# GNN on one core: in the edge groups without counts, the highest score's broadcast and the exponentials move one group ahead of the weighting, and the order of work on ScalarE and TensorE changes

## The chip, the cores and the metric

One core of a Trainium2 chip runs the whole program in one launch. The metric is the device time in microseconds, median of the runs.

## The reference, cut to what matters

A graph attention layer over 6250 nodes and 200000 edges (sorted by destination), then a residual node update, then four graph convolutions over the same edges. The part around the change is the attention and the first nodes' update:

```
ft = (hn @ W_att).reshape(n, 10, 13)
scores = einsum('ehd,ehd->eh', ft[src], ft[dst]) / sqrt(13)
m = segment_max(scores, dst);  ex = exp(scores - m[dst])
z = segment_sum(ex, dst);      a = ex / z[dst]
agg = segment_sum(ft[src] * a[:, :, None], dst)
out = elu(agg) @ hr_w + hr_b + hn
out = layernorm(out); skip2 = out
out = elu(elu(out @ w1 + b1) @ w2 + b2) + skip2
```

## The kernel before

**Groups.** `attention` cuts the edges into 196 groups of 1024 (8 columns of 128). One loop body per engine is run for k = 0 to 195 plus LAG = 3 more (`steps`); each body works on several groups at once: `nxt` = k+1, `one` = k-1, `two` = k-2, `late` = k-3, `over` = k-4. I call body k "pass k". Engines meet at semaphores only, and each works through its own list in order. GpSimd gathers the source rows of a group with eight indirect DMAs into one of six `fts` buffers; the gathers of group n wait for the weighting of group n-6.

**What one group goes through.** TensorE: `nearness` (a distance between edge and node, one matmul), ScalarE: `destination_rows` (a Relu that makes the one-hot `ohdT`), TensorE: `closeness` (the same, turned, into the same PSUM bank), ScalarE: `destination_columns` (the one-hot `oh`), TensorE: `first_features` and `last_features` (rows of the destinations, `ftd_ps`), VectorE: `first_products`, `last_products` (product with the gathered rows, the reduction to scores, and the running highest score), TensorE: `turn_highest`, VectorE: `highest` (one number for the group), TensorE: `broadcast_highest` (to all partitions, `spread`), ScalarE: `numerators` (copy of the shift, Exp into PSUM, fade, Exp into `terms`), VectorE: `weighted` (gathered rows times exponentials), TensorE: `first_sums`, `later_sums`, `carried`, `last_sum` into `agg_ps`, ScalarE: `result`, and a store by SP.

**Two kinds of group.** Passes 0 to 175 (`counted`, k < NSD = 176) also count edges into the adjacency strips. Passes 176 to 198 have no counts; in their place they carry the fused update of the first 14 node tiles. That is cut into four units with 17 phases, `units_at(k, 0)` being the pieces in the first place of a pass and `units_at(k, 1)` those in the second; the units begin at slots 0, 5, 15, 20 of two slots a pass, so the last piece falls in pass 194. TensorE has work in phases 2, 3 (turns), 4 (`project`, three matmuls a tile), 7 (turn), 8 to 11 (`up`), 12 (`down`), 13 and 16 (turns). Behind each `up` ScalarE takes an Exp (`exp_cols`) and VectorE an elu (`elu_quarter`), and the next `up` needs that elu, since it uses the same bank. Phases 5 and 14 are `deviation` (a Sqrt on ScalarE, which needs another activation table than Exp) and `coefficients` on VectorE.

**Order within a pass without counts, before.** TensorE: broadcast of k-3, turn of k-2, nearness of k+1, first piece, closeness, first and later sums of k-3, last features of k-1, last sums of k-3, first features of k, second piece. ScalarE: numerators of k-3, destination rows of k+1, result of k-4, first piece, destination columns of k+1, second piece. VectorE, which isn't changed: weighting of k-3, first products of k-1, highest of k-2, first piece, last products of k-1, second piece.

Of the kernel before, what the change touches and what calls it, by code (L numbers as in the profile page):

```python
# [5 lines left out]
F32 = mybir.dt.float32  # L6
# [3 lines left out]
ACT = mybir.ActivationFunctionType  # L10
# [3 lines left out]
P = 128  # L14
# [56 lines left out]
NSD = T0 * P // SUB  # L71
# [705 lines left out]
def attention(nc, t, sb, pb, sem, g):  # L777
# [15 lines left out]
    LAG = 3  # L793
# [5 lines left out]
    with ExitStack() as c:  # L799
# [33 lines left out]
        s2T = [sb(f"fu_s2T{a}", [D, UW * P], F32, c) for a in range(2)]  # L833
        uT = [a[:].rearrange("p s n k -> p (s n k)").bitcast(F32)[:, 0:4 * UW * P].rearrange("p (f n) -> p f n", f=4)
              for a in (ohk, ohl)]
        st, mv = sb("fu_st", [P, 2, UW, 6], F32, c), sb("fu_mv", [P, 2, UW, 2], F32, c)
        sd, rs, nb = (sb("fu_" + n, [P, 2, UW], F32, c) for n in ("sd", "rs", "nb"))
        adj_ps = [pb(f"adj_ps{q}", [P, 512], F32, c) for q in range(2)]
# [52 lines left out]
        def units_at(k, half):  # L891
            slot = 2 * (k.n - SLOTS_AT) + half
            return [(Unit(i), slot - first) for i, first in enumerate(STARTS) if 0 <= slot - first < PHASES]
# [311 lines left out]
        def _(act):  # L1205
            act.wait_ge(iotas, 1)

            def low_distances(k):

                own = low_cols[:, k.n].rearrange("p a c -> p (a c)")  # L1210
                if k.after(2):
                    act.wait_ge(dist_l_done, k.n - 1)
                nc.scalar.copy(low[:, k.s, :], own[:, LD:NA * SC]).then_inc(lows_done, 1)  # L1213
                if k.after(1):
                    act.wait_ge(ohl_done, k.n)
                act.wait_ge(lows_done, k.n + 1)
                for n in range(NA * SC - LD):
                    last = nc.scalar.activation(dist_l[:, n, :], lo_iota[:], ACT.Abs, bias=low[:, k.s, n:n + 1], scale=-1.0)  # L1218
                last.then_inc(dist_l_done, 1)
# [22 lines left out]
            def numerators(k):  # L1242

                act.wait_ge(spread, k.n + 1)
                nc.scalar.copy(shift[:, k.s, :], most_ps[:, P:P + 2]).then_inc(shift_done, 1)
                act.wait_ge(shift_done, k.n + 1)
                if k.after(1):
                    act.wait_ge(terms_done, k.n)
                nc.scalar.activation(most_ps[:, EX_AT:EX_AT + GC * H], score[:, k.c, 0:GC * H], ACT.Exp,  # L1249
                                     bias=shift[:, k.s, 0:1], scale=RS).then_inc(exp_done, 1)  # L1250
                if k.after(1):
                    nc.scalar.activation(fade[:, k.s, 0:1], shift[0:WD, k.s, 0:1], ACT.Exp,
                                         bias=shift[0:WD, 1 - k.s, 1:2]).then_inc(fade_done, 1)
                if k.after(2):
                    act.wait_ge(agg_done, k.n - 1)
                nc.scalar.activation(terms[:, k.s, :, HD:HD + H],
                                     score[:, k.c, 0:GC * H].rearrange("p (c h) -> p c h", h=H), ACT.Exp,
                                     bias=shift[:, k.s, 0:1], scale=RS).then_inc(kept_done, 1)

            def result(k):  # L1260

                act.wait_ge(agg_done, k.n + 1)
                if k.after(UN):
                    act.wait_ge(agg_out, 16 * (k.n - UN + 1))
                nc.scalar.copy(res[:, k.u, :], agg_ps[0:WD, 0:WA]).then_inc(res_done, 1)
# [23 lines left out]
            def deviation(k, var, done):  # L1289
                act.wait_ge(var, k.i + 1)  # L1290
                nc.scalar.activation(sd[:, k.a, 0:k.w], mv[:, k.a, 0:k.w, 1], ACT.Sqrt, bias=eps[:]).then_inc(done, 1)

            def normal(k):
                act.wait_ge(f["nb1"], k.i + 1)
# [28 lines left out]
            def nodes(k, phase):  # L1323
                if phase == 1:
                    exp_attention(k)
                elif phase == 2:
                    copy_attention(k)
                elif phase == 3:
                    copy_rest(k)
                elif phase == 5:  # L1330
                    deviation(k, f["var1"], f["sd1"])
                elif phase == 6:
                    normal(k)
                elif phase == 7:
                    scaled_cols(k)
                elif 8 <= phase < 12:
                    exp_cols(k, f["up_ps"], 4 * k.i + phase - 7, b1[:, phase - 8:phase - 7], f["exF"])
                elif phase == 12:
                    exp_cols(k, f["v_ps"], k.i + 1, b2[:], f["exV"])
                elif phase == 14:  # L1340
                    deviation(k, f["var2"], f["sd2"])
                elif phase == 15:
                    rectified(k)
                elif phase == 16:
                    hT_out(k)

            def body(k):
                nxt, late, over = k.at(1), k.at(-LAG), k.at(-LAG - 1)
                if k.counted():
                    if k.after(2):  # L1350
                        act.wait_ge(strip_out[k.s], 16 * (k.j * (UN // 2) + k.u // 2))
                    copy_quarter(k, 0)
                if late.exists():
                    numerators(late)
                if nxt.exists():
                    destination_rows(nxt)
                if k.counted():
                    copy_quarter(k, 1)
                if over.exists():
                    result(over)  # L1360
                for unit, phase in units_at(k, 0):
                    nodes(unit, phase)
                if nxt.exists():
                    destination_columns(nxt)
                for unit, phase in units_at(k, 1):
                    nodes(unit, phase)
                if k.counted():
                    copy_quarter(k, 2)
                if nxt.counted():
                    low_distances(nxt)  # L1370
                    low_one_hots(nxt)
                if k.counted():
                    copy_quarter(k, 3)
                    act.wait_ge(strip_done, 4 * k.n + 4)
                    act.dma_start(adj[k.n],
                                  strip[:, k.s].rearrange("p t a d -> p (t a d)")).then_inc(strip_out[k.s], 16)
            zero = Group(0)
            low_distances(zero)
            low_one_hots(zero)
# [5 lines left out]
        def _(pe):  # L1385
# [83 lines left out]
            def later_sums(k):  # L1469
                add_terms(k, range(HC, GC - 1))  # L1470
# [80 lines left out]

            def body(k):
                nxt, one, two, late = k.at(1), k.at(-1), k.at(-2), k.at(-LAG)
                if late.exists():
                    broadcast_highest(late)
                if two.exists():
                    turn_highest(two)
                def last_sums():
                    if late.after(1):
                        carried(late)  # L1560
                    last_sum(late)

                def counted():
                    count(k, 0)
                    if nxt.exists():
                        nearness(nxt)
                    count(k, 1)
                    count(k, 2)
                    if one.exists():
                        last_features(one)  # L1570
                    if nxt.exists():
                        closeness(nxt)
                    count(k, 3)
                    if late.exists():
                        first_sums(late)
                        later_sums(late)
                    first_features(k)
                    if late.exists():
                        last_sums()

                def uncounted():
                    if nxt.exists():
                        nearness(nxt)
                    for unit, phase in units_at(k, 0):
                        nodes(unit, phase)
                    if nxt.exists():
                        closeness(nxt)
                    first_sums(late)
                    later_sums(late)
                    if one.exists():  # L1590
                        last_features(one)
                    last_sums()
                    if k.exists():
                        first_features(k)
                    for unit, phase in units_at(k, 1):
                        nodes(unit, phase)
                if k.counted():
                    counted()
                else:
                    uncounted()  # L1600
# [1233 lines left out]
```

## Time and profile before

| | |
|---|---|
| median of 3 runs | 3775.62 us (3770.89 to 3781.33) |
| profiled execution, its time | 3790.5 us |
| its span | 3788.6 us |
| mean granted TensorE clock | 0.892 |
| busy: PE, DVE, ACT, POOL | 89%, 62%, 47%, 65% |
| gathers of the attention stage (L1001) | 118.5 to 2076.4 us |

The stages stand one behind the other with a barrier between: a prelude to about 118 us, attention to about 2118 us, the rest of the node update, and the convolutions from between 2250 and 2300 us. Times in the trace count from the start of the span; a line number is that of the kernel before.

### The profile page before, as it was taken

To read this page: it belongs to the slowest core of one execution; us is meant where nothing else is said; L and a number is where in the kernel's file an instruction comes from. 1 tells how busy PE (TensorE), PEld (TensorE's weight loads), DVE (VectorE), ACT (ScalarE), POOL (GpSimd) and SP (SyncE) were. 2 spreads that over 40 slices of the span, in tenths; PEclk is the share of its full clock that TensorE was granted. 3 is DMA by queue.
4 is the path that set the end of the run, shared out by engine and by line. 5 is a ranking of instruction groups with operands and counts; after the bars stand their busy time and mean duration, and the time that the engine had idled before them with its cause. 6 is when DMAs were issued, how large, how long until landed. Compare 5 with 4: busy or idle time off the path is not lost. (4 is left out here: it accounts for less than half of the span.)

```text
span 3788.6 us, 59184 instructions
## 1 busy us (share of the span) xinstructions
PE 3354.5 (89%) x20346; PEld 2097.6 (55%) x20346; DVE 2355.1 (62%) x3512; ACT 1776.8 (47%) x4853; POOL 2445.6 (65%) x2604
## 2 busy tenths in 40 slices
PE   5788888888888888888888787999999999999999
PEld 4566666666666666666655554444544454445444
DVE  8788888888888888888865574222422242224223
ACT  4788888888888878787744353000200020002000
POOL 2577777777777777777777001777277737764775
PEclk7688888888888888888887798999999999999999
DMA  7443334333333333334332415888688868877886
GB/s 207 125 108 103 107 104 107 104 107 104 107 104 107 104 107 104 107 104 124 103 85 60 62 51 169 254 254 256 215 255 254 253 215 254 256 248 229 259 264 192
DMA packets 491674, 599.98 MB, mean 158 GB/s; under 512 B 61546, under 2 KB 422613, under 8 KB 491103
## 3 DMA queue, kind: packets, MB, share of 16 engines
q1 hardware_dynamic: 355798, 337.71, 29.3%
q0 software_dynamic: 82960, 172.57, 18.4%
q10 hardware_dynamic: 52632, 86.13, 6.3%
q8 instruction: 152, 2.49, 0.3%
q14 instruction: 132, 1.07, 0.1%
HBM read 488.79 MB, written 109.00 MB: 158 GB/s over the span
## 5 line engine op out<-in xcount | busy, mean ns | idle before, releaser
L1001 POOL DMA_INDIRECT fts<-ft_tab,src_all x1568 | 1481.2, 945 | 477.7 <-issue 477.1
L2702 PE MATMUL cv_acc<-cv_cnt,cv_parts 128*128 128x512 bf16 x3960 | 864.0, 379 | 0.0
L2453 POOL DMA_INDIRECT cv_slots<-hs_tab,slot_idx x640 | 604.8, 945 | 195.1 <-issue 195.1
L1033 DVE TENSOR_TENSOR ohk<-iota_ps,key_cols 128x784 bf16<-128x784 f32 x704 | 651.1, 966 | 5.5
L2702 PEld LDWEIGHTS cv_acc<-cv_cnt,cv_parts 128*128 128x128 bf16 x3960 | 387.2, 98 | 464.6
L1457 PE MATMUL agg_ps<-terms,oh 128*64 128x141 f32 x2744 | 557.1, 378 | 75.6 <-DVE terms L1070 75.3
L1457 PEld LDWEIGHTS agg_ps<-terms,oh 128*64 128x64 f32 x2744 | 483.2, 189 | 116.3 <-DVE terms L1070 105.4
L1218 ACT ACTIVATE dist_l<-lo_iota,low 128x128 bf16<-128x128 f16 x1760 | 533.1, 387 | 16.5 <-ACT low L1213 0.4
L1397 PE MATMUL adj_ps<-ohk,ohl 128*128 128x196 bf16 x2816 | 378.2, 261 | 89.5 <-ACT strip L1270 46.8
L1270 ACT CAST strip<-adj_ps 128x392 bf16<-128x392 f32 x704 | 334.0, 474 | 239.5 <-PE adj_ps L1400 200.4
L2702 PE MATMUL cv_acc<-raw,cv_parts 128*128 128x512 bf16 x1920 | 420.9, 379 | 0.0
L1047 DVE TENSOR_TENSOR prod<-ftd_ps,fts 128x780 f32<-128x780 f32 (+1 forms) x392 | 271.0, 691 | 225.9 <-DMA fts<-ft_tab,src_all 198.4
L1423 PE MATMUL ftd_ps<-win,ohdT 64*128 64x130 f32 x3136 | 325.8, 334 | 77.7 <-DVE prod L1047 76.4
L2453 POOL DMA_INDIRECT spare<-hs_tab,slot_idx x320 | 302.6, 946 | 97.5 <-issue 97.5
L1397 PEld LDWEIGHTS adj_ps<-ohk,ohl 128*128 128x128 bf16 x2816 | 215.2, 100 | 221.7 <-DVE ohk L1033 109.5
L1423 PEld LDWEIGHTS ftd_ps<-win,ohdT 64*128 64x128 f32 x3136 | 244.3, 219 | 157.3 <-DVE prod L1047 90.1
L2702 PEld LDWEIGHTS cv_acc<-raw,cv_parts 128*128 128x128 bf16 x1920 | 187.7, 98 | 226.7
L2669 ACT ACTIVATE cv_sd<-cv_mv,eps 128x1 f32<-128x1 f32 x2 | 0.6, 294 | 662.0 <-DVE cv_tmp L2620 662.0
L2514 DVE TENSOR_REDUCE spare<-cv_slots 128x128 f32<-128x1152 f32 x50 | 106.5, 2130 | 303.0 <-DMA cv_slots<-hs_tab,slot_idx 302.9
L1070 DVE TENSOR_TENSOR terms<-fts,most_ps 128x1040 f32<-128x1040 f32 x196 | 240.9, 1229 | 21.5 <-ACT most_ps L1249 21.2
L1083 DVE TENSOR_REDUCE score<-prod 128x80 f32<-128x1040 f32 x196 | 242.4, 1237 | 6.7
L1225 ACT ACTIVATE ohl<-dist_l 128x1280 bf16<-128x1280 bf16 x176 | 223.5, 1270 | 16.3 <-ACT dist_l L1218 0.4
(350 smaller groups left out, 3592.1 us busy)
## 6 DMA issues: line engine op xcount, KB each, us to landing
cv_cnt<-adj SPq DMA_DIRECT2D x44, 2176.0 KB
cv_cnt<-adj SPq DMA_DIRECT2D x44, 2048.0 KB
raw<-adj SPq DMA_DIRECT2D x44, 2048.0 KB
adj<-strip ACTq DMA_DIRECT2D x176, 392.0 KB
fts<-ft_tab,src_all POOLq DMA_INDIRECT x1568
win<-ft_tab SPq DMA_DIRECT2D x196, 65.0 KB
hs_tab<-cv_hs ACTq DMA_DIRECT2D x24, 448.0 KB, 3.5
cv_slots<-hs_tab,slot_idx POOLq DMA_INDIRECT x640
```

The source lines that it names most:

```text
L1001: nc.gpsimd.indirect_dma_start(fts[u][:, k, :], None, ft_tab[:, :], bass.IndirectOffsetOnAxis(src_all[:, n, k:k + 1], 0)).then_inc(gathere ...
L1033: nc.vector.tensor_tensor(ohk[:, k.s, at, :], key_no.unsqueeze(1).to_broadcast([P, QC, KEYS]), columns(key_cols, k)[:, at].unsqueeze(2).to ...
L1047: nc.vector.tensor_tensor(by_half(prod[:]), ftd_ps[:, :, 0:n * HD].rearrange("p a (c f) -> p a c f", f=HD), by_half(fts[k.f][:]), ALU.mult ...
L1070: nc.vector.tensor_tensor(terms[:, k.s, :, 0:HD].rearrange("p c (h d) -> p c h d", d=DH), fts[k.f][:].rearrange("p c (h d) -> p c h d", d=DH),
L1083: nc.vector.tensor_reduce(score[:, k.c, 0:GC * H], prod[:].rearrange("p c (h d) -> p (c h) d", d=DH), AX.X, ALU.add).then_inc(score_done, 1)
L1218: last = nc.scalar.activation(dist_l[:, n, :], lo_iota[:], ACT.Abs, bias=low[:, k.s, n:n + 1], scale=-1.0)
L1270: nc.scalar.copy(strip[:, k.s, :, QS * q:QS * (q + 1), :].rearrange("p t a d -> p a t d"), adj_ps[q % 2][:, 0:QS * KEYS].rearrange("p (a t ...
L1397: nc.tensor.matmul(counts_ps[:, a * KEYS:(a + 1) * KEYS], ohl[:, k.s, n, :], ohk[:, k.s, n, :], start=(a == 0 and m == 0), stop=False)
L1423: last = nc.tensor.matmul(ftd_ps[:, half, m * HD:(m + 1) * HD], ohdT[at, k.u, (c0 + m) * P:(c0 + m + 1) * P], win[at, k.u, :], start=True, ...
L1457: nc.tensor.matmul(agg_ps[0:WD, 0:WA], oh[:, k.o, col, half, :], terms[:, k.s, n, :], start=(n == 0), stop=False)
L2453: nc.gpsimd.indirect_dma_start(slots[n % RING][:, e, :], None, hs_tab[:, :], bass.IndirectOffsetOnAxis(rows_at, 0)).then_inc(slots_in[n % ...
L2702: last = nc.tensor.matmul(a[:, 0:width], parts[:, r, b, :], cnt[q][:, 0:width // SUB, (b - b0) * SUB:(b - b0 + 1) * SUB], start=(b == 0 an ...
```

## The change

In passes without counts only: TensorE broadcasts the highest score of group k-2 in pass k, behind the sums and the first piece, and ScalarE makes that group's numerators in pass k between the two pieces. Pass 176, the first of its kind, does both group 173 and group 174. On ScalarE the destination rows come first, then the result and the destination columns, then the first piece. On TensorE closeness follows nearness, then the first and later sums, the first piece, the broadcast, the last features, the last sums, the second piece, and the first features. An Exp on one column (`warm`) follows each Sqrt of `deviation`. Passes with counts keep their order; VectorE, GpSimd and SP are as before.

```diff
--- before.py
+++ after.py
@@ -833,6 +833,7 @@
         s2T = [sb(f"fu_s2T{a}", [D, UW * P], F32, c) for a in range(2)]
         uT = [a[:].rearrange("p s n k -> p (s n k)").bitcast(F32)[:, 0:4 * UW * P].rearrange("p (f n) -> p f n", f=4)
               for a in (ohk, ohl)]
+        warm = sb("fu_warm", [P, 1], F32, c)
         st, mv = sb("fu_st", [P, 2, UW, 6], F32, c), sb("fu_mv", [P, 2, UW, 2], F32, c)
         sd, rs, nb = (sb("fu_" + n, [P, 2, UW], F32, c) for n in ("sd", "rs", "nb"))
         adj_ps = [pb(f"adj_ps{q}", [P, 512], F32, c) for q in range(2)]
@@ -1289,6 +1290,7 @@
             def deviation(k, var, done):
                 act.wait_ge(var, k.i + 1)
                 nc.scalar.activation(sd[:, k.a, 0:k.w], mv[:, k.a, 0:k.w, 1], ACT.Sqrt, bias=eps[:]).then_inc(done, 1)
+                nc.scalar.activation(warm[:], eps[:], ACT.Exp)
 
             def normal(k):
                 act.wait_ge(f["nb1"], k.i + 1)
@@ -1345,35 +1347,46 @@
                     hT_out(k)
 
             def body(k):
-                nxt, late, over = k.at(1), k.at(-LAG), k.at(-LAG - 1)
-                if k.counted():
+                nxt, two, late, over = k.at(1), k.at(-2), k.at(-LAG), k.at(-LAG - 1)
+
+                def counted():
                     if k.after(2):
                         act.wait_ge(strip_out[k.s], 16 * (k.j * (UN // 2) + k.u // 2))
                     copy_quarter(k, 0)
-                if late.exists():
-                    numerators(late)
-                if nxt.exists():
+                    if late.exists():
+                        numerators(late)
                     destination_rows(nxt)
-                if k.counted():
                     copy_quarter(k, 1)
-                if over.exists():
-                    result(over)
-                for unit, phase in units_at(k, 0):
-                    nodes(unit, phase)
-                if nxt.exists():
+                    if over.exists():
+                        result(over)
                     destination_columns(nxt)
-                for unit, phase in units_at(k, 1):
-                    nodes(unit, phase)
-                if k.counted():
                     copy_quarter(k, 2)
-                if nxt.counted():
-                    low_distances(nxt)
-                    low_one_hots(nxt)
-                if k.counted():
+                    if nxt.counted():
+                        low_distances(nxt)
+                        low_one_hots(nxt)
                     copy_quarter(k, 3)
                     act.wait_ge(strip_done, 4 * k.n + 4)
                     act.dma_start(adj[k.n],
                                   strip[:, k.s].rearrange("p t a d -> p (t a d)")).then_inc(strip_out[k.s], 16)
+
+                def uncounted():
+                    if k.n == NSD:
+                        numerators(late)
+                    if nxt.exists():
+                        destination_rows(nxt)
+                    result(over)
+                    if nxt.exists():
+                        destination_columns(nxt)
+                    for unit, phase in units_at(k, 0):
+                        nodes(unit, phase)
+                    if two.exists():
+                        numerators(two)
+                    for unit, phase in units_at(k, 1):
+                        nodes(unit, phase)
+                if k.counted():
+                    counted()
+                else:
+                    uncounted()
             zero = Group(0)
             low_distances(zero)
             low_one_hots(zero)
@@ -1551,7 +1564,7 @@
 
             def body(k):
                 nxt, one, two, late = k.at(1), k.at(-1), k.at(-2), k.at(-LAG)
-                if late.exists():
+                if late.exists() and k.n <= NSD:
                     broadcast_highest(late)
                 if two.exists():
                     turn_highest(two)
@@ -1581,19 +1594,20 @@
                 def uncounted():
                     if nxt.exists():
                         nearness(nxt)
-                    for unit, phase in units_at(k, 0):
-                        nodes(unit, phase)
-                    if nxt.exists():
                         closeness(nxt)
                     first_sums(late)
                     later_sums(late)
+                    for unit, phase in units_at(k, 0):
+                        nodes(unit, phase)
+                    if two.exists():
+                        broadcast_highest(two)
                     if one.exists():
                         last_features(one)
                     last_sums()
+                    for unit, phase in units_at(k, 1):
+                        nodes(unit, phase)
                     if k.exists():
                         first_features(k)
-                    for unit, phase in units_at(k, 1):
-                        nodes(unit, phase)
                 if k.counted():
                     counted()
                 else:
```

## Rows read from the trace of the kernel before

**Rows 1.** The page, the granted clock in 40 equal slices of the span, in tenths of full speed.
```profile
PEclk7688888888888888888887798999999999999999
```

**Rows 2.** One line's instructions: duration min/median/max in ns, first and last start.
```profile
L1001 POOL DMA_INDIRECT fts<-ft_tab,src_all x1568: 940/944/1278, 118.5 to 2076.4; - x196
```

**Rows 3.** Timeline of VectorE (start, us, engine, line, operation [idle before <-releaser]).
```profile
1918.06 0.97 DVE L1047 TENSOR_TENSOR prod<-ftd_ps,fts 128x780 f32<-128x780 f32 x1 [2.67 <-DMA fts<-ft_tab,src_all]
...
2098.36 0.95 DVE L1047 TENSOR_TENSOR prod<-ftd_ps,fts 128x780 f32<-128x780 f32 x1
```

**Rows 4.** Stretches: length, busy us of PE, PEld, DVE, ACT, POOL, clock, DMA, GB/s.
```profile
1918.10:2114.70 196.60, 166.48 (x934) 112.78 (x934) 114.66 (x244) 80.07 (x196) 120.84 (x127) 0.79 0.29 68
...
1945.10:1956.60 11.50, 10.10 (x63) 5.93 (x62) 9.22 (x24) 5.20 (x11) 8.76 (x10) 1.00 0.43 108
...
1992.60:2006.80 14.20, 11.93 (x58) 8.22 (x56) 6.63 (x18) 9.07 (x21) 10.85 (x12) 0.50 0.27 64
```

**Rows 5.** Waits of TensorE from 1918 to 2115 (us in total, times, longest).
```profile
PE agg_ps L1457 <- DVE terms L1070: 6.8, 6, 1.9
PE near_ps L1415 <- ACT ohdT L1233: 6.3, 4, 2.2
PE ftd_ps L1423 <- DVE prod L1047: 4.9, 5, 1.8
...
PE adj_ps L1518 <- DVE ohl L1141: 2.7, 3, 1.4
...
PE adj_ps L1518 <- DVE ohk L1141: 1.6, 2, 0.9
...
PE adj_ps L1524 <- DVE ohk L1141: 1.1, 1, 1.1
...
PE adj_ps L1524 <- DVE ohl L1141: 0.9, 1, 0.9
```

**Rows 6.** Timeline, the steps of the loop without a piece.
```profile
1885.34 0.39 PE L1410 MATMUL near_ps<-rows,spots 5*128 5x512 f16 x1
...
1885.78 0.58 ACT L1233 ACTIVATE ohdT<-near_ps 128x512 f32<-128x512 f32 x1
...
2094.04 0.58 PE L1423 MATMUL ftd_ps<-win,ohdT 64*128 64x130 f32 x4
...
2095.30 0.94 PE L1423 MATMUL ftd_ps<-win,ohdT 64*128 64x130 f32 x12
...
2096.17 0.38 PE L1444 MATMUL most_ps<-signs,most 1*128 1x2 f32 x2
...
2096.44 0.24 DVE L1088 TENSOR_REDUCE score<-score 128x1 f32<-128x81 f32 x1
...
2098.43 1.91 PE L1457 MATMUL agg_ps<-terms,oh 128*64 128x141 f32 x14 [1.32 <-DVE terms L1070]
...
2107.04 0.62 PE L1475 MATMUL agg_ps<-res,move 64*1 64x140 f32 x2
...
2108.13 0.38 PE L1444 MATMUL most_ps<-signs,most 1*128 1x2 f32 x2
```

**Rows 7.** Timeline, an up piece and its elu, and fourteen sums at half clock.
```profile
1961.71 1.12 PE L1518 MATMUL adj_ps<-fu_s2T,spare 128*128 128x512 f32 x2
...
1964.06 0.75 DVE L1141 SCALAR_TENSOR_TENSOR ohl<-adj_ps,spare,ohk 128x512 f32<-128x512 f32 x1
...
1905.41 3.55 PE L1457 MATMUL agg_ps<-terms,oh 128*64 128x141 f32 x14
```

**Rows 8.** ScalarE: groups of table loads from 1878 to 2112, and one in the timeline.
```profile
L1291 ACT ACT_TABLE_LOAD x8 | 10.3, 1283 | 0.1
...
L1249 ACT ACT_TABLE_LOAD x4 | 5.1, 1283 | 0.1
...
1902.24 1.28 ACT L1249 ACT_TABLE_LOAD   x1
...
1903.54 0.33 ACT L1249 ACTIVATE most_ps<-score,shift 128x80 f32<-128x80 f32 x1
```

## The prediction

> **What bounds the kernel now.** I read the profile's page first: the granted clock of TensorE swings over the attention stage, the first 22 of 40 slices, and is steady behind it [rows 1]. The edit touches only the groups without counts, so I looked for that stretch: groups 176 to 195 and three passes of the loop behind them. The gathers on GpSimd come first: 1568 of them, the first at 118.5 us and the last at 2076.4 us, with hardly a wait for anything but their own queue [rows 2]. That is 1957.9 / 1567 = 1.25 us each, 10.0 us for a group's eight. While a pass of the loop takes under 10 us, gathers set its rhythm. Then I followed the first products of each group on VectorE. Those of group 179 wait for their gather and start at 1918.06. Those of group 195 could start 0.7 us behind the last gather (1918.06 against 1917.4 is that 0.7: 16 groups of 10.0 us back from 2077.3), at 2078.0, but start at 2098.36 [rows 3]. In 16 passes the loop has fallen **20.3 us** behind, and what bounds the kernel from 1918.1 to the end of the last copy of `res` at 2114.7 [rows 4] is the ring of TensorE, ScalarE and VectorE, not the gathers. Those 20.3 us, and 1.1 us behind the last group (below), are all that an order of work can win.
>
> Of these 196.6 us TensorE is busy for 166.5 us, at a mean granted clock of 0.79 of 2.4 GHz. Single passes stand at 1.00 (11.5 us for one with a `down`) and others at 0.50 (14.2 us for the one from 1992.6) [rows 4]. It is idle for 196.6 - 166.5 = 30.1 us. The list of waits names most of that: 6.8 us for the weighted terms, 6.3 us for `ohdT`, 4.9 us for the products, and 2.7 + 1.6 + 1.1 + 0.9 = 6.3 us for the elu pieces of VectorE [rows 5].
>
> **The change, part by part.** No matmul goes or comes; TensorE's 166.5 us stay, and only idle time can move. I count in passes 181 to 194 (14 of them), where the loop is late.
>
> *Highest score and exponentials a group ahead.* `broadcast_highest` used to open the pass. From it to the first sum 2098.43 - 2096.17 = 2.26 us go by (copy of the shift, exponentials, weighting) [rows 6]. Now the exponentials of group k-2 are there before pass k+1 begins, so the wait for the terms in this form is gone: **6.8 us won**. Behind the last group, its last sums (8.13 - 7.04 us, carried row included) fit between broadcast and weighting instead of standing ahead of the broadcast: **1.1 us won** (2107.04 and 2108.13 are starts in [rows 6]).
>
> *`destination_rows` first on ScalarE.* It no longer stands behind the three exponentials and their table load: **6.3 us won**. But `closeness` now follows `nearness` at once, with nothing between. Nearness starts at 1885.34, the Relu at 1885.78 for 0.58 us: with 0.05 us to wake TensorE, closeness can't start before 1.07 us, of which nearness itself fills about 0.35 [rows 6]. That is 0.7 us idle in each of 14 passes, which before lay under the pieces or under the exponentials: **9.8 us lost**.
>
> *Pieces of the fused node update behind the sums.* Nearly the whole pass's sums now lie between the second piece of one pass and the first of the next, so the 6.3 us of waits for the elu at those places go, and with `first_features` behind the second piece also the 4.9 us for the products: **11.2 us won**. The price is at the other side. First and second piece now have only the broadcast (0.3 us), the last features and last sums (2095.30 - 2094.04 = 1.26 us, so 1.5 us in all) between them, while the way through ScalarE and VectorE takes from the end of an up piece (1961.71 + 1.12 = 1962.83) to the end of the elu (1964.81), 2.0 us, and 2.1 with the wake-up [rows 6, 7]: 0.6 us in the nine late passes in which both places hold such a piece (181 to 184, 188 to 192): **5.4 us lost**. VectorE's order is unchanged, so the elu of the first piece delays the last products, score and its maximum, and these gate `turn_highest`, which now has no broadcast ahead of it: from the last features 2096.44 + 0.24 - 2094.04 = 2.64 us, against 2.07 us of last sums and first features [rows 6]: 0.6 us where no second piece covers it, in about five passes: **3.0 us lost**. And the elu of the second piece stands on VectorE ahead of `weighted`: 2.1 + 1.24 us from that piece's end to the terms, against first features 0.87, a turn of about 0.3, 1.07 from nearness to closeness and closeness about 0.4, 2.6: 0.7 us in eight passes: **5.6 us lost**.
>
> *The `warm` activation.* The number of table loads stays: each of the eight at `deviation` is followed by one back, four of these ahead of the exponentials (5.1 us, [rows 8]); that one now follows at once. Where `deviation` is a first piece, ScalarE has nothing else to do: nothing, under the sums (1.9 us and more). As second piece it now puts 2 x 1.28 us of loads, the Sqrt and the Exp (0.33 us at most, as the wider one of 128x80 in [rows 8]), some 3.1 us, ahead of the next Relu. The four-matmul project covers that in pass 185, in 188 and 190 first features, turn and nearness (some 1.5 us) and the 0.7 already counted cover it only in part, and ScalarE also has an elu's Exp (0.69) there: I take 2.1 us for 188, where the Exp stands ahead of the loads, and 0.6 for 190, where it stands behind them and the broadcast's own 1.3 us overlap: **2.7 us lost**. If the last features covered it too, nothing.
>
> What a switch of tables costs is read from one of these loads: it starts at 1902.24, and the Exp behind it at 1903.54, so 1.3 us with everything [rows 8]. The Trainium skill (ScalarE: Activation LUTs, What ACT_TABLE_LOAD costs) counts a drain on top, 2.66 us in all. The trace disagrees, and decides. By the page the four loads ahead of exponentials would weigh some 5 us more before and those in passes 188 and 190 some 3 us more after, and the sum would fall by about 2 us.
>
> **The sum.** Won 6.8 + 1.1 + 6.3 + 11.2 = 25.4 us, lost 9.8 + 5.4 + 3.0 + 5.6 + 2.7 = 26.5 us: +1.1 us. Against the profiled execution (3790.5 us, span 3788.6) that is 3791.6. That execution is 14.9 us above the median of the runs, all of it in stages that I can't tell apart, so I carry the difference over: 3775.6 + 1.1 = **3776.7**, say 3777 us. The ends of the unknown terms: if the losses that I inferred from order alone (5.4, 3.0, 5.6, 2.7) were nothing, the sum is -15.6 us; if each were double, +17.8 us.
>
> **Rivals.**
> *The ring catches up (faster).* The 25.4 us are won, the new waits fall together, and TensorE, with no stop of over 1 us, holds 2.4 GHz: the pass from 1992.6 stood at half clock [rows 4], where 14 sums take 3.55 against 1.91 us [rows 6, 7]. Then the loop is as fast as the gathers: 20.3 + 1.1 us off, 3754; half of that is 3765. For: the waits are named in the profile. Against: a new wait lies ready behind each. Chance 0.17.
>
> *VectorE in order plus the clock (slower).* `weighted` and the last products stand behind elu pieces; stops of 2 us appear in passes 182 to 185, of which the one shown ran at 1.00 before, and the granted clock falls there to 0.50. A pass then costs 3.55 - 1.91 = 1.6 us more in its sums [rows 6, 7], and its other matmuls on the ring (last features and sums 1.26, first features 0.87, a piece 1.12, closeness 0.4: 3.65 us), lengthened in the same proportion and taken at two thirds of it since parts of them are covered, 2.1 us: 3.7 us, in three or four passes 11 to 15 us: 3788 to 3792. [...] For: the pass at 0.50 from 1992.6 has one of TensorE's waits of up to 2.2 us for `ohdT` ahead of it, behind a table load [rows 4, 5]. Against: the first sums follow at once. Chance 0.13.
> The Trainium skill (TensorE: Matmul & The Clock Gate, HAM oscillation — how this bites in real kernels) says that bursts of matmuls with waits between are run throttled again and again. The pass at 0.50 bears that out; by this rule the slower case would be the likely one.
>
> *It does nothing to the ring.* If the passes depend only on TensorE's own work and the waits just change their names, only the 1.1 us at the end remain: 3774.5. Chance 0.10, no change in any measurement.
>
> **How the numbers follow.** Forecast 0.60, nothing 0.10, faster 0.17, slower 0.13. Over 0.3%, 11.3 us, is what this kernel can tell from no change. So faster 0.17, same 0.70, slower 0.13. The range leaves a tenth at each end: down to half way into the catching-up case (3763), up to the lower end of the slower one (3789). The likeliest case alone is 3767 to 3786.
>
> **What would show it.** Right: the first products of group 195 still start 15 to 25 us behind the last gather; TensorE waits in the list for `ohdT` in nearly every pass, about 0.7 us each; the wait of `agg_ps` for terms is still there, now behind elu pieces; no table load stands at the exponentials' line; ring time from broadcast to first sum is no longer fixed at 2.3 us. The gathers still end within 1 us of 2077.3. Wrong: the last gather's group is multiplied within 8 us of its landing (the ring was won), or the granted clock of 1945 to 1980 is below 0.8 and the stage ends behind 2126 (slower case). A difference outside 1870 to 2120 us would mean something that I haven't seen.

## The result, and the profile after

The changed kernel takes 3792.9 us (median of 6 runs, 3787.6 to 3795.4) against 3776.4 us: ratio **1.0042, 95% interval 1.0028 to 1.0055**. It is slower by 16.4 us, beyond the upper end of the range (3789) and 1 us above the price of the slower rival (3788 to 3792). Ratios leave out single executions far above all others (4015 us of the kernel before, 10449 us of e13_more_filler, 5878 us of e15_ahead_filler).

The page of the changed kernel shows the granted clock of [rows 1] at this grain but for the first slice, and a span only 1.4 us longer than the 3788.6 us of the trace that the prediction rests on:

```profile
span 3790.0 us, 59192 instructions
...
PEclk8688888888888888888887798999999999999999
```

So the comparison of these two traces shows less than a tenth of the difference of the medians. That is the first thing to explain. Gathers, one line of the changed kernel (it is [rows 2] one line further down), with what they waited for:

```profile
L1002 POOL DMA_INDIRECT fts<-ft_tab,src_all x1568: 939/945/1203, 117.1 to 2079.9; - x196
...
  DVE terms L1071: 5.9, 3
```

The last gather starts 3.5 us later than before, and three gathers now wait 5.9 us in all for a buffer (two waited 0.6 us before): the loop has fallen back as far as six buffers allow. VectorE's first products of groups 179 and 195, and the last copy of `res`, in the timeline (as [rows 3]):

```profile
1917.82 0.95 DVE L1048 TENSOR_TENSOR prod<-ftd_ps,fts 128x780 f32<-128x780 f32 x1
...
2104.66 0.96 DVE L1048 TENSOR_TENSOR prod<-ftd_ps,fts 128x780 f32<-128x780 f32 x1
...
2117.38 0.27 ACT L1266 COPY res<-agg_ps 64x141 f32<-64x141 f32 x1 [3.38 <-PE agg_ps L1494]
```

The first products of group 195 start at 2104.66, 6.3 us later than before, and the copy ends at 2117.65 instead of 2114.65: from group 195's products to the end it is 13.0 us instead of 16.3. The end of the chain became shorter, the passes before it longer.

Stretches of the changed kernel (columns as in [rows 4]): group 180's first products to the end, two passes with fused pieces early on, and one at half clock:

```profile
1931.50:2117.68 186.18, 152.27 (x880) 101.56 (x877) 106.30 (x227) 81.73 (x196) 109.42 (x115) 0.83 0.27 64
1942.43:1959.57 17.14, 13.67 (x63) 8.34 (x63) 8.96 (x23) 6.02 (x12) 12.97 (x14) 0.80 0.37 88
1959.57:1972.64 13.07, 10.18 (x49) 6.15 (x49) 7.90 (x18) 6.96 (x17) 9.93 (x11) 0.76 0.42 99
...
2007.23:2019.19 11.96, 11.89 (x50) 8.00 (x50) 5.25 (x11) 2.84 (x9) 9.15 (x10) 0.50 0.31 65
```

TensorE is idle for 186.18 - 152.27 = 33.9 us of the first. Its waits, from 1918 to 2118 (as [rows 5]):

```profile
PE near_ps L1428 <- ACT ohdT L1234: 13.9, 15, 2.7
PE agg_ps L1470 <- DVE terms L1071: 11.4, 13, 1.9
PE agg_ps L1464 <- DVE score L1089: 3.8, 6, 1.4
PE ftd_ps L1436 <- DVE prod L1048: 2.0, 1, 2.0
...
PE adj_ps L1531 <- DVE ohk L1142: 1.0, 2, 0.6
PE adj_ps L1531 <- DVE ohl L1142: 0.9, 2, 0.5
PE adj_ps L1537 <- DVE ohl L1142: 0.6, 1, 0.6
```

The waits for `ohdT` doubled (6.3 to 13.9 us), those for terms went from 6.8 to 11.4, those for the maximum from 1.2 to 3.8. The waits for elu pieces shrank from 6.3 to 1.0 + 0.9 + 0.6 = 2.5 us and those for products from 4.9 to 2.0; that they shrink was forecast. How a pass comes to take 17.1 us is seen in its timeline:

```profile
1941.21 1.23 DVE L1071 TENSOR_TENSOR terms<-fts,most_ps 128x1040 f32<-128x1040 f32 x1
1941.74 0.60 PE L1428 MATMUL near_ps<-spots,rows 5*128 5x128 f16 x4 [1.85 <-ACT ohdT L1234]
...
1942.50 3.55 PE L1470 MATMUL agg_ps<-terms,oh 128*64 128x141 f32 x14 [0.15 <-DVE terms L1071]
...
1945.98 4.87 PE L1537 MATMUL adj_ps<-ohk,spare 128*128 128x512 f32 x8
...
1957.31 0.39 PE L1428 MATMUL near_ps<-spots,rows 5*128 5x128 f16 x4 [0.69 <-ACT ohdT L1234]
...
1958.36 1.23 DVE L1071 TENSOR_TENSOR terms<-fts,most_ps 128x1040 f32<-128x1040 f32 x1
```

Closeness (L1428) has waited 1.85 us for the Relu and starts at 1941.74. The sums (L1470) follow in 3.55 us: half clock, as in [rows 7]. The `down` behind them (L1537) takes 4.87 us. With the clock up again, closeness starts again at 1957.31, the weighting stands on VectorE behind the second piece's elu until 1958.36, and the next sums start only at 1959.64.

### The profile page after: what moved, and what is told of

It reads as the page before. It is cut to its first block and busy times, and to the rows that moved or that the text cites. A ratio compares the mean times of both kernels' runs of the same rounds, so it can differ in the third digit from the quotient of the medians.

```text
span 3790.0 us, 59192 instructions
## 1 busy us (share of the span) xinstructions
PE 3352.7 (88%) x20346; PEld 2093.9 (55%) x20346; DVE 2353.7 (62%) x3512; ACT 1782.7 (47%) x4861; POOL 2446.4 (65%) x2604
## 5 line engine op out<-in xcount | busy, mean ns | idle before, releaser
L1470 PE MATMUL agg_ps<-terms,oh 128*64 128x141 f32 x2744 | 556.9, 378 | 77.0 <-DVE terms L1071 77.0
L1470 PEld LDWEIGHTS agg_ps<-terms,oh 128*64 128x64 f32 x2744 | 483.2, 189 | 118.1 <-DVE terms L1071 106.8
L1226 ACT ACTIVATE ohl<-dist_l 128x1280 bf16<-128x1280 bf16 x176 | 223.5, 1270 | 16.3 <-ACT dist_l L1219 0.4
```

The lines of the kernel that those rows point to most:

```text
L1470: nc.tensor.matmul(agg_ps[0:WD, 0:WA], oh[:, k.o, col, half, :], terms[:, k.s, n, :], start=(n == 0), stop=False)
```

## The experiments

**A second trace of each kernel.** The kernel before, without an edit (e1_before), and the changed one (e2_after).

> The kernel before, once more, for a second trace: the profiled execution of before (3790.5 us) lies 14 us above its own median, so its trace may not show the typical run. Theory A (the change costs what the order of work costs, 10 to 16 us within passes 176 to 198): the ratio is 1.000, and if this trace is of a run near 3776 us, group 195's first products start 10 to 15 us earlier than the 2098.4 us of the first trace. Rival B (the loss lies outside the edited stretch, by the layout of memory or code): group 195's first products stay near 2098 us, and the 14 us lie elsewhere.

> The changed kernel once more. Both theories: ratio about 1.004. Theory A: its first products of group 195 again start at 2104 to 2110 us, and the last copy of res ends at 2117 to 2123. Rival B: those times move little, and a later stage is longer than in before.

The kernel before against itself, 12 runs: 1.0013 (1.0001 to 1.0025), 3771.9 to 3793.7 us: that interval misses 1, so differences of 0.1% mean nothing here. Its trace again was from a longer execution (3785.3 us), with passes equal to the first trace's within 0.1 us. The changed kernel: 1.0035 (1.0022 to 1.0048), five runs within 2.5 us; last copy of `res` from 2114.8. It repeats (11 runs within 8 us), and the kernel before does so less: its runs spread over 26 us.

**What the spread of the kernel before is.** No edit again (e10_before, e11_before).

> The kernel before, for one more trace. Its runs lie between 3767 and 3794 us, both traces so far at 3785 and 3790, and over 50 runs a lower mean granted clock goes with a longer time. If the clock in the late passes makes the difference: a trace near 3770 us ends its attention stage 10 to 15 us earlier than 2114, with fewer passes at 0.50. If another stage does, this trace's passes are as long as in the first.

> As e10_before: one more trace of the kernel before, to have traces from both ends of its spread.

They took 3775.3 and 3773.5 us, one execution each, and end their last copy at 2096.6 and 2098.9. The stretch from group 180's first products to the end, in the first trace:

```profile
1934.27:2114.68 180.41, 151.92 (x880) 103.17 (x879) 106.99 (x227) 77.67 (x189) 108.36 (x114) 0.81 0.28 65
```

and in that of e10_before:

```profile
1927.86:2096.58 168.72, 138.31 (x875) 94.53 (x875) 106.88 (x227) 76.99 (x189) 112.39 (x118) 0.90 0.31 71
```

The same matmuls take 138.3 us at a mean clock of 0.90 and 151.9 us at 0.81 (875 and 880 records of them), and idle time differs by 2 us (30.4 and 28.5). The rest of the kernel, from the end of that stretch to the end of the span, is 1673.9 us in the first trace, 1676.8 in e10_before and 1672.3 in the changed kernel's. So the 14.9 us between my trace and the median lay in the late passes, and rival B falls: the loss is in the edited stretch. Over 117 runs of the kernel before, time and mean granted clock correlate at -0.8; the fastest quarter has its median at 3770.7 us and 0.898, the slowest at 3784.5 and 0.894.

These traces also correct what bounds the kernel. The first products of group 195 in e10_before:

```profile
2078.49 0.97 DVE L1047 TENSOR_TENSOR prod<-ftd_ps,fts 128x780 f32<-128x780 f32 x1
```

Its last gather starts at 2075.1 and ends 0.9 us later, so by the prediction's reckoning (0.7 us behind the gather's end) these products are 1.8 us late, and those of e11_before also 1.8 us (2081.2 against 2079.4). The 20.3 us of the first trace belong to its longer execution. In a run near the median the loop falls behind in the fused passes too, but has caught up with the gathers by group 195.

**The first piece ahead of the sums again** (e3_piece_ahead). Only TensorE's order differs from the changed kernel:

```diff
                         nearness(nxt)
-                        closeness(nxt)
-                    first_sums(late)
-                    later_sums(late)
                     for unit, phase in units_at(k, 0):
                         nodes(unit, phase)
+                    if nxt.exists():
+                        closeness(nxt)
+                    first_sums(late)
+                    later_sums(late)
                     if two.exists():
                         broadcast_highest(two)
```

> The changed kernel with the first piece of TensorE back between nearness and closeness; all else as in the changed kernel. Theory A, the stop between nearness and closeness (0.7 us in 14 passes) and the piece right ahead of the last features cost: 6 to 12 us faster than the changed kernel, ratio to before 1.001 to 1.003. Rival C, the exponentials a group ahead or ScalarE's order cost instead: as slow as the changed kernel, 1.004. Rival B: 1.004.

3767.2 us, **0.9972** (0.9960 to 0.9984): 23 us faster than the changed kernel and faster than the one before. Theory A expected 6 to 12, so its price was far too low; rivals B and C, which expected no gain, fall. The stretch and two of its waits:

```profile
1930.39:2093.31 162.92, 135.56 (x880) 92.06 (x879) 105.90 (x226) 80.82 (x196) 111.15 (x117) 0.92 0.29 74
```

```profile
PE near_ps L1428 <- ACT ohdT L1234: 3.2, 4, 1.6
...
PE agg_ps L1470 <- DVE terms L1071: 4.9, 6, 1.1
```

Against the changed kernel the waits fall to 3.2 and 4.9 us, idle time by 33.9 - 27.3 = 6.6 us, and busy time by 152.3 - 135.6 = 16.7 us at a clock of 0.92. The `down` with closeness and the sums behind it:

```profile
1937.92 3.70 PE L1537 MATMUL adj_ps<-ohk,spare 128*128 128x512 f32 x8 [1.28 <-DVE ohk L1142]
...
1941.99 0.39 PE L1428 MATMUL near_ps<-spots,rows 5*128 5x128 f16 x4
1942.31 1.90 PE L1470 MATMUL agg_ps<-terms,oh 128*64 128x141 f32 x14
```

The piece fills the time in which ScalarE makes `ohdT`. Closeness has nothing to wait for here, and the sums run at 1.90 us. Other waits came in their place, 5.2 + 1.3 + 0.3 + 0.2 = 7.0 us for elu pieces against 2.1 in this stretch of the changed kernel. At its end e3 too has caught up with the gathers (group 195's products at 2079.2, last gather from 2075.9).

**Useless work in the stop** (e9_filler). In the changed kernel, between nearness and closeness:

```diff
                         nearness(nxt)
+                        for _ in range(2):
+                            nc.tensor.matmul(iota_ps[:, 0:P], ident[:], ident[:], start=True, stop=True)
                         closeness(nxt)
```

> The changed kernel with two useless 128x128 matmuls of fp32 between nearness and closeness in the 19 passes where nearness exists; they fill TensorE's stop for ohdT with work (some 0.8 us, the stop was 0.7 us at the least) and add nothing that is used. Theory G (the order costs time mainly through the granted clock, which falls behind stops): the mean clock from group 180's first products to the end rises from 0.83 to 0.88 or more, and the kernel is no slower than the changed one, likely 3 to 10 us faster. Theory A in its plain form (stops cost only their own length): 0 to 4 us slower.

3778.8 us, 1.0001 (0.9990 to 1.0013): **about 12 us faster than the changed kernel by doing more**. Stretch, and the wait at closeness, in its trace (of an execution 6 us above its median):

```profile
1927.98:2111.50 183.52, 157.32 (x932) 105.86 (x929) 106.49 (x227) 81.55 (x196) 113.91 (x119) 0.85 0.28 66
```

```profile
PE near_ps L1428 <- ACT ohdT L1234: 3.8, 3, 2.1
```

The waits of 12.6 us became 3.8 us; the matmuls that fill them can save nothing of them by themselves. The useless ones are 10.3 us of the 157.3, so the useful ones take 147.0 us instead of 152.3: that is what the clock gave back. The trace has it at 0.85, less than the 0.88 that I expected, and its stretch is only 2.7 us shorter than the changed kernel's. The size of the gain, 12 us, rests on the medians and ratios; this trace shows its direction. The order is as in the changed kernel, so the late terms stay: 11.8 us.

**More of it** (e13_more_filler): the same two matmuls once more, between closeness and the first sums.

> The changed kernel with two useless 128x128 matmuls between nearness and closeness and two more ahead of the first sums, in 19 passes. Theory G (stops of TensorE cost mainly through the granted clock): as fast as e9 or faster, ratio 0.998 to 1.001. Theory A in its plain form, or G exhausted by e9 since closeness to sums is no stop in every pass: the second pair costs its own 0.4 to 0.8 us a pass, 5 to 12 us slower than e9, 1.002 to 1.004.

1.0011 (1.0002 to 1.0021), 3781.1 us. No win over e9, and no clear loss either: 2 us by the medians and 4 by the ratios, with intervals that overlap. Plain cost would have been 5 to 12.

```profile
1929.03:2103.35 174.32, 152.60 (x988) 105.28 (x985) 105.29 (x227) 81.43 (x196) 112.06 (x118) 0.93 0.30 69
```

Clock 0.93 in the trace, the highest of all, with 988 records of matmuls instead of 880. The useless ones are 19.7 us of the 152.6, the useful ones 132.9, so the second pair wins back a good part of what it costs.

**The same filler where it should do nothing** (e14_before_filler, e15_ahead_filler): ahead of closeness in the kernel before and in e3.

> The kernel before with two useless 128x128 matmuls ahead of closeness in 19 passes. If its own spread (3767 to 3794 us) comes from the granted clock in the late passes, the filler keeps the clock up: narrower spread, median 3768 to 3774, 0.998 to 0.999. If the clock in before depends on something that these stops don't touch: 0 to 8 us slower, 1.000 to 1.002, with the same spread.

> e3 (first piece between nearness and closeness) with the same filler ahead of closeness. Its late passes are near the gathers' 10.0 us and its clock is at 0.92, so little is left to win: within 4 us of e3, 0.996 to 0.999. If the useless work is now on the ring: 5 to 10 us slower, 0.999 to 1.000.

Before with filler: 0.9999 (0.9990 to 1.0008), where 0.998 to 0.999 would have shown that these stops pull its clock down. Its runs lie from 3771 to 3783 us, those of the kernel before beside them from 3770 to 3785: neither the median nor, clearly, the spread moved. The stop ahead of closeness isn't shown to be what makes the kernel before slow in some executions. e3 with filler: 0.9983 (0.9974 to 0.9992), 2 to 4 us slower than e3 and within what was expected: there the clock was up already.

**Closeness between the halves of the sums** (e5_closeness_later), in the changed kernel:

```diff
                         nearness(nxt)
-                        closeness(nxt)
                     first_sums(late)
+                    if nxt.exists():
+                        closeness(nxt)
                     later_sums(late)
```

> The changed kernel with closeness behind the first half of the sums instead of right behind nearness; the first piece stays behind the sums. Theory A (the stop between nearness and closeness costs: 12.6 us of waits for ohdT in the trace of the changed kernel): those waits fall below 4 us and the kernel is 8 to 12 us faster than the changed one, ratio 1.000 to 1.002. Theory E (what costs is that the first piece stands right ahead of the broadcast and the last features, so that VectorE's last products, score and maximum come late): 3 us or less faster, 1.003 or more.

3814.9 us, 1.0099 (1.0073 to 1.0124), 24 us slower than the changed kernel. Both theories were wrong. The trace is of the longest of its six executions (3829.4 us). The same stretch, waits from 1918 to 2156, and the gathers:

```profile
1945.42:2155.75 210.33, 175.35 (x881) 113.41 (x881) 106.20 (x227) 81.41 (x196) 98.42 (x104) 0.72 0.22 53
```

```profile
PE agg_ps L1470 <- DVE terms L1071: 21.2, 12, 3.0
PE agg_ps L1470 <- ACT res L1266: 7.9, 6, 3.0
```

```profile
L1002 POOL DMA_INDIRECT fts<-ft_tab,src_all x172 | 162.9, 947 | 91.0 <-issue 49.4 <-DVE terms L1071 41.6
```

The wait for `ohdT` is gone, but the sums now come right behind nearness and wait for `result`, which stands behind the Relu on ScalarE (7.9 us, new), and for terms (21.2). Idle time is 210.3 - 175.4 = 35.0 us, near the changed kernel's 33.9: the waits only moved. What grew is the time of the same matmuls, 175.4 us at a clock of 0.72 against 152.3 at 0.83, and the loop falls so far back that gathers wait 41.6 us for buffers. A stop can't be judged by its name.

**VectorE's last products first** (e6_products_first): `last_products` ahead of the first piece, in the changed kernel.

```diff
+                if one.exists():
+                    last_products(one)
                 for unit, phase in units_at(k, 0):
                     nodes(unit, phase)
-                if one.exists():
-                    last_products(one)
```

> The changed kernel with VectorE's last products, scores and maximum ahead of its first piece in passes without counts. Theory E: the maximum comes 1 us earlier in ten passes, and the kernel is 6 to 12 us faster than the changed one, ratio 1.001 to 1.002. Theory A: the second piece of TensorE waits as much longer for the first piece's elu, and the stop between nearness and closeness stays: within 4 us of the changed kernel, 1.003 to 1.005.

3832.6 us, 1.0154 (1.0131 to 1.0176). The elu of the first piece now waits behind products and scores, and with it TensorE's second piece (waits from group 179's first products, 1918.9, to 2134.0):

```profile
PE near_ps L1428 <- ACT ohdT L1234: 13.9, 15, 3.1
PE adj_ps L1531 <- DVE ohk L1142: 7.2, 3, 2.5
PE adj_ps L1531 <- DVE ohl L1142: 7.0, 3, 3.8
PE adj_ps L1544 <- DVE fu_cols L1149: 6.1, 2, 3.2
```

Theory E's gain did not come, and A's "within 4 us of the changed kernel" didn't hold either: this order is some 42 us slower. The late maximum costs 3.8 us in the changed kernel, so little could be won there; the way from piece to piece is dear.

**Without `warm`** (e4_no_warm from the changed kernel, e7_ahead_no_warm from e3).

```diff
-                nc.scalar.activation(warm[:], eps[:], ACT.Exp)
```

> The changed kernel without the warm Exp behind each Sqrt. Theory A: the loads back return to the exponentials, which are no longer on the ring, and the two exposed loads (2.7 us by the sum) go: 0 to 3 us faster than the changed kernel, 1.003 to 1.004. Rival D, the two table loads in a row ahead of the destination rows are the main cost: 8 us or more faster, 1.002 or less.

> The kernel with the first piece between nearness and closeness (e3_piece_ahead, 0.9972), without the warm Exp. In the changed kernel leaving it out won about 4 us (1.0035 to 1.0023). If the two loads in a row delay the destination rows as there: 2 to 5 us faster than e3, 0.996. If the load back now stands ahead of an up piece's Exp on the ring: 1 to 4 us slower, 0.998.

From the changed kernel: 1.0023 (1.0013 to 1.0033), 4 us by the ratios and 6 by the medians faster than e2 on the same chip, where I had expected 0 to 3. Rival D (8 us or more) falls. Stretch and waits in its trace, of the fastest of its 11 executions (3776.9 us; they go up to 3791.8):

```profile
1926.98:2101.45 174.47, 141.00 (x877) 95.23 (x877) 105.65 (x225) 77.44 (x187) 112.76 (x119) 0.90 0.28 69
```

```profile
PE agg_ps L1469 <- DVE terms L1071: 13.1, 14, 1.9
PE near_ps L1427 <- ACT ohdT L1234: 10.9, 13, 1.6
```

`ohdT` costs 10.9 instead of 12.6 us, terms 13.1 instead of 11.4. Idle time is 174.5 - 141.0 = 33.5 us, as in the changed kernel's 33.9, and yet the clock is 0.90 and the stretch 11.7 us shorter: with the stops still there, an execution of nearly the same order kept its clock. From e3: 0.9984 (0.9973 to 0.9995), 2 us slower by the medians and 4 by the ratios. Both differences are of the size by which the kernel before differs from itself (1.0013), so neither the worth of `warm` nor that its sign depends on the order is shown.

**Rows first alone** (e8_rows_first): the kernel before with `destination_rows` ahead of `numerators` in passes without counts.

> The kernel before, with only ScalarE's destination rows put ahead of the numerators in passes without counts. Theory A: TensorE's waits for ohdT (6.3 us in its trace) nearly go, but the exponentials come 0.6 us later in each pass and with them the terms and the sums: within 5 us of the kernel before, 0.999 to 1.001. Rival F, the rows first are what wins in e3: 0.998 or less.

1.0018 (1.0006 to 1.0031), 7 us slower by the ratio, where A said within 5 us (1.001 at most). Rival F falls: there is no gain. The wait moves and grows:

```profile
PE agg_ps L1459 <- DVE terms L1070: 16.4, 11, 2.6
...
PE near_ps L1417 <- ACT ohdT L1233: 1.6, 3, 0.7
```

1.6 us for `ohdT` instead of 6.3 (6.9 to 7.2 in the traces of e10 and e11), but 16.4 us for terms instead of 6.8.

**First features ahead of the second piece** (e12_features_ahead), in e3:

```diff
+                    if k.exists():
+                        first_features(k)
                     for unit, phase in units_at(k, 1):
                         nodes(unit, phase)
-                    if k.exists():
-                        first_features(k)
```

> e3 (first piece between nearness and closeness) with first_features ahead of the second piece, as in the kernel before. If first features behind the second piece help (their operands' wait for VectorE's last products, 4.9 us in the trace of before, is covered): 2 to 6 us slower than e3, 0.998 to 0.999. If they only delay the next group's products: 0 to 4 us faster, 0.996 to 0.997.

1.0012 (1.0000 to 1.0024): 13 to 15 us slower than e3, where I expected 2 to 6. The products' wait is back near the 4.9 us of [rows 5], but between the two traces idle time in the stretch grew by 1.1 us only and busy time by 8.0 us (143.6 us at 0.86 against 135.6 at 0.92):

```profile
PE ftd_ps L1436 <- DVE prod L1048: 5.0, 5, 2.8
```

## Why the prediction was wrong

**The base.** The step that failed is the last of the sum, the base that it was added to: the 14.9 us between the profiled execution and the median were "all of it in stages that I can't tell apart, so I carry the difference over". They lay in the very passes that the change touches. Two traces of the kernel before had a clock of 0.81 there and two had 0.89 and 0.90, 14 to 18 us apart at the end of the stage. Against the trace that I had, the sum was near: +1.1 us forecast, +3.0 us at the last copy of `res`. That nearness is in part luck: idle time moved by more than the sum said (below), while the pass of group 180 fell from 16.2 to 13.7 us. Against e10_before the changed kernel's stretch is 186.2 - 168.7 = 17.5 us longer, which is the 16.4 us of the medians.

**What there was to win.** "Those 20.3 us, and 1.1 us behind the last group, are all that an order of work can win" holds for the profiled execution alone. In the traces near the median 1.8 us of lag are left, so there was next to nothing to win in the loop and much to lose.

**"TensorE's 166.5 us stay, and only idle time can move."** Wrong for the same reason. Of those 17.5 us, 152.3 - 138.3 = 14.0 are busy time of the same matmuls at another clock, and 33.9 - 30.4 = 3.5 are idle. A sum of waits could not hold the larger part. The changed kernel is at 0.83 in both traces and its runs lie within 8 us: it has lost what the kernel before has in its better runs.

**The terms of the sum.** Waits for terms, 5.6 us forecast in the changed kernel: measured 11.4 in 13 waits, where I had counted eight: sized at half of what it is. In the timeline above it is the second piece's elu that stands ahead, as forecast. Waits for `ohdT`, 9.8 + 2.7 = 12.5: measured 12.6 in the late passes and 13.9 from 1918 on, right in sum. Waits of pieces for the elu, 5.4: measured 2.5, too high. Products, nothing: 2.0. Maximum, 1.2 + 3.0: 3.8, right. The end behind the last products, 1.1 us won: it is 3.3 us shorter in the traces. In sum, idle time in the stretch moved by 5.4 us against my first trace, not by 1.1.

**The rivals.** The slower rival named the kind of cause (elu pieces ahead of `weighted`, stops, then a lower clock) and nearly the size (11 to 15 us, 3788 to 3792), and I gave it 0.13. The place it had only in part: passes 182 to 185 are 6.9 us longer than in e10_before, passes 187 to 192 another 17.0, and the end behind group 195's products is 5.1 us shorter. Of its passes 182 and 183 came out at 0.80 and 0.76 instead of 0.50. e3 and e9 bear the cause out: without the stop, or with useless work in it, 23 and 12 us go. The Trainium skill (TensorE: Matmul & The Clock Gate, HAM oscillation — how this bites in real kernels), which I had put beside that rival, says that bursts of matmuls with waits between are run throttled again and again. The changed kernel agrees (0.80, 0.76, and 0.50 from 2007.2 on, in a stretch at 0.83); e4's trace, 0.90 with the same idle time, does not. The catching-up rival was right for e3's order against my trace: its stretch ends 21.4 us before that one, the 20.3 + 1.1 us of that rival. Against e10_before it ends only 3.3 us earlier.

**The signs to look for.** Group 195's products 15 to 25 us behind the last gather: 2104.66 - 2080.9 - 0.7 = 23.1, held. Waits for `ohdT` in nearly every pass: 15 of them, held. No table load at the exponentials' line: held. Gathers' end within 1 us of 2077.3: 2080.9, not held, since the lag met the six buffers. Clock from 1945 to 1980 below 0.8: 0.81 (0.84 in e2_after; 0.97 in the first trace), not held. The range's lower end, 3763, was called half way into the catching-up case; by the sum half way is 3765. Stage end behind 2126: not held, because that bound too was counted from one of the longer executions.

What stays open: what sets the clock in one execution. Total idle time doesn't: in this stretch 28.5 us went with 0.81 and 30.4 with 0.90 in the kernel before, 33.9 with 0.83 in the changed one and 33.5 with 0.90 without `warm`. So it isn't known why the kernel before has two patterns, and e14 did not settle it. e5's 24 us are read from one trace, not taken apart by a run of their own.

## What to carry to other kernels

Where engines wait for each other in a ring, an order of work is judged by what TensorE has to do while another engine makes its next operand: put independent work whose operands are ready between the request and the use (here a node piece between nearness and closeness). Work that waits itself won't do: the first sums in the same place, in e5, cost 24 us. Before carrying a difference to the median, compare the trace's time with the median; if it lies apart by more than the effect, take several traces and see whether the difference lies in the stretch that is to be changed. And compare the busy time and granted clock of the same matmuls as well as the waits: here most of each difference lay in the former.

## What was unexpected of the hardware

Two useless 128x128 matmuls in each of 19 passes made the changed kernel some 12 us faster (3790.5 to 3778.8 us; each against the kernel before on its own chip, 1.0035 and 1.0001). The same 880 matmul records took 152.3 us at a mean granted clock of 0.83 in the changed kernel and 135.6 us at 0.92 with one piece of work moved, though TensorE's idle time differs by only 6.6 us. And one program, unchanged, had passes equal within 0.1 us in two executions and late passes 12 us shorter in two others: the clock made two patterns of it, 0.81 and 0.90.
